# Two idle PSUM banks take the third and fourth down products; the routing runs unbroken on VectorE

## The reference

```python
def _L0_ffn_ref(x, Wr, br, Wgate, bgate, W1, W3, W2):    # x: (10000, 512), normed
    tw = _routing_weights(xf, Wr, br, Wgate, bgate)      # (N, 16)
    for e in range(16):                                  # W1, W3: 512 x 32, W2: 32 x 512
        h = silu(xf @ W1[e]) * (xf @ W3[e])
        out = out + tw[:, e:e + 1] * (h @ W2[e])

# _routing_weights: softmax over 4 groups, and in each group softmax over 4 experts;
# keep the top 2 of each (the second only while the cumulated share is <= 0.9),
# renormalise, multiply group by expert weight, times 0.5
```

## Time and profile before

| | |
|---|---|
| median of 3 runs | 2429.84 us |
| profiled execution, its own time | 2421.65 us |
| span of its instructions | 2419.9 us |
| PE busy | 2269.3 us (94%), 10550 matmuls |
| VectorE busy | 1794.4 us (74%) |
| ScalarE busy | 1150.4 us (48%) |
| GpSimd busy | 675.4 us (28%) |
| mean granted PE clock | 0.969 |

### The profile page before, as it was taken

How to read it: one execution, slowest core, us unless ns; L and a number is a source line. 1 busy time by engine, 2 the same in 40 slices (tenths; PEclk the granted TensorE clock), 3 DMA queues, 4 the chain that set the end, 5 groups by cost and what they waited for, 6 DMA issues and landing times. The chain is left out here.

```text
span 2419.9 us, 33046 instructions
## 1 busy us (share of the span) xinstructions
PE 2269.3 (94%) x10550; PEld 1815.3 (75%) x10550; DVE 1794.4 (74%) x4258; ACT 1150.4 (48%) x2136; POOL 675.4 (28%) x624
## 2 busy tenths in 40 slices
PE   6799986899999999999789999999997899999998
PEld 4577665688888888888668888888876677777776
DVE  8588796888888888886556755555566688888886
ACT  7565322445445454454442222222235767667652
POOL 6455022222122221210222221222233334333320
PEclk9899987999999999999899999999998899999999
DMA  5211133132231322311443344333356566666631
GB/s 166 60 54 53 19 127 104 60 98 89 69 105 60 99 88 70 105 53 49 158 161 126 125 146 134 129 129 133 130 160 202 112 181 153 148 175 159 152 109 48
DMA packets 155872, 271.87 MB, mean 112 GB/s; under 512 B 35538, under 2 KB 36178, under 8 KB 155478
## 3 DMA queue, kind: packets, MB, share of 16 engines
q1 hardware_dynamic: 123014, 203.00, 25.0%
q0 software_dynamic: 32720, 67.19, 12.8%
HBM read 185.82 MB, written 100.41 MB: 118 GB/s over the span
## 5 line engine op out<-in xcount | busy, mean ns | idle before, releaser
L2415 ACT ACTIVATE conv_h<-conv_h 128x512 f32<-128x512 f32 x79 | 50.0, 632 | 306.1 <-DVE conv_h L2344 306.1
L2892 POOL DMA_INDIRECT next_own<-message,net_slot_d x75 | 125.4, 1672 | 149.7 <-DMA next_own<-own 132.3
L2313 DVE TENSOR_TENSOR conv_yl<-conv_pty,conv_yh 128x512 fp32r<-128x512 f32 x79 | 54.6, 691 | 149.0 <-ACT conv_yh L2405 141.0
L68 PE MATMUL conv_p<-conv_w_hi,conv_yh 128*128 128x512 f32 x316 | 132.4, 419 | 1.6 <-DVE conv_yl L2313 1.6
L68 PE MATMUL d_po<-shared_wq_hi,d_hh 128*128 128x512 f32 x316 | 129.5, 410 | 2.6 <-DVE rows_rows L1523 0.2
L1373 POOL TENSOR_TENSOR d_rs<-d_ve,net_half_neg 128x4 f32<-128x4 f32 x37 | 37.3, 1007 | 337.0 <-DVE d_ve L1431 283.8
L68 PE MATMUL d_pc<-d_xh,shared_wv_hi 128*128 128x512 f32 (+1 forms) x320 | 128.6, 402 | 0.0
L68 PE MATMUL d_pa<-d_xh,xp_w_hi 128*128 128x512 f32 (+1 forms) x320 | 128.1, 400 | 0.0
L70 PE MATMUL conv_p<-conv_w_hi,conv_yl 128*128 128x512 f32 x316 | 126.5, 400 | 0.0
L69 PE MATMUL conv_p<-conv_w_lo,conv_yh 128*128 128x512 f32 x316 | 126.2, 399 | 0.0
L70 PE MATMUL conv_p<-conv_w_hi,conv_hl 128*128 128x512 f32 x316 | 125.6, 397 | 0.0
(11 more groups left out here) (621 smaller groups left out, 7173.4 us busy)
## 6 DMA issues: line engine op xcount, KB each, us to landing
conv_yin<-y SPq DMA_DIRECT2D x79, 256.0 KB, 2.7
h<-conv_h SPq DMA_DIRECT2D x79, 256.0 KB, 2.0
own<-xp_own_buf SPq DMA_DIRECT2D x79, 256.0 KB, 2.0
next_own<-own SPq DMA_DIRECT2D x79, 256.0 KB, 4.5
next_x<-y SPq DMA_DIRECT2D x79, 256.0 KB, 2.9
out<-d_res SPq DMA_DIRECT2D x79, 256.0 KB, 2.6
y<-d_y SPq DMA_DIRECT2D x78, 256.0 KB, 2.2
d_x<-in_x SPq DMA_DIRECT2D x10, 1024.0 KB, 7.4
```

The costliest lines, as they stand in the source:

```text
L68: te.matmul(out, lhs[0], rhs[0], start=first, stop=False, skip_group_check=True)
L2313: v.tensor_tensor(lo[:, t % 2, :], bank[t % 2][:], hi[:, t % 2, :].bitcast(F32), ALU.subtract)\
L2415: act_.activation(h[:, t, :], h[:, t, :], ACT.Relu).then_inc(h_made, 1)
L2892: pool.indirect_dma_start(own[n][:, t, :], None, k.message2[:, :], bass.IndirectOffsetOnAxis(ap=k.slot["d"][:, T * g + t:T * g + t + 1], a ...
```

## The change

The third and fourth tile's down products go to `pc[1]` and `pa[1]`. The down products of tiles 2 and 3 lose their wait for `back`; those of tiles 0 and 1 wait for `back` of the same tile of the group before; and `up` of chunk 1 with `w1` gets a wait for all four `back`s of the group before. On VectorE the routing is in one piece, apart from `front1` and `front1_end`, and the four `back`s follow.

```diff
+        down_bank = [po[0], po[1], pc[1], pa[1]]
...
-                v.scalar_tensor_tensor(x[u][:, t, :], x[u][:, t, :], 1.0, po[t % 2][:], ALU.mult, ALU.add,
+                v.scalar_tensor_tensor(x[u][:, t, :], x[u][:, t, :], 1.0, down_bank[t][:], ALU.mult, ALU.add,
                                        accum_out=row_sum[:, t:t + 1]).then_inc(x2_made, 1)
...
-                    def first_back():
-                        back(g, u, 0)
-                        if front:
-                            front1(i, c_ + 2)
-
-                    between = {7: first_back, 9: lambda: back(g, u, 1)}
-                    if front:
-                        between[15] = lambda: front1_end(g + 2)
-                    routing(g + 1, between)
-                    back(g, u, 2)
-                    back(g, u, 3)
+                    routing(g + 1, {7: lambda: front1(i, c_ + 2), 15: lambda: front1_end(g + 2)} if front else {})
+                    for t in range(T):
+                        back(g, u, t)
...
+                if name == "w1" and cc == 1 and g:
+                    pe.wait_ge(x2_made, 4 * g + 2)
...
-                    if cc == 0:
-                        pe.wait_ge(x2_made, 4 * g + t + 1)
+                    if cc == 0 and g and t < 2:
+                        pe.wait_ge(x2_made, 4 * g - 4 + t + 1 + 2)
                     pe.wait_ge(hl_made, 4 * g + cc + 1 + 2)
-                    last = split3(pe, po[t % 2][:], (hh[:, cc, sl], hl[:, cc, sl]),
+                    last = split3(pe, down_bank[t][:], (hh[:, cc, sl], hl[:, cc, sl]),
                                   (w["w2"][0][:, cc, :], w["w2"][1][:, cc, :]), cc == 0, cc == KC - 1)
```

## The result

The changed kernel took 2416.14 us in the median of four runs (2414.22 to 2418.13), against 2430.35 us for the kernel before on the same chip (2429.34 to 2432.61). The ratio is 0.9943, with an interval of 0.9930 to 0.9957. The medians differ by 14.2 us. The forecast was 2419.0 us, or -10.8.

The account below looks back on a forecast made before the run. PE was taken as the bound, busy 94% of the span and waiting for VectorE twice per group. Only those waits counted, -10.8 us, the other terms nothing: 2429.84 - 10.8 = 2419.0 us, range 2415.5 to 2424.5.

Parts of the forecast that it names:

- (a): First expert stage: PE's two waits per group at the down products of tiles 2 and 3 go, -10.8 us.
- (b): VectorE: without two `back`s the routing ends 1.2 us earlier; cost nothing, 1.1 us to spare at `turn_mix`.
- (c): VectorE: four `back`s in a row behind the routing cost nothing; 0.9 to 1.0 us idle left at `w3`.
- (d): PE's new wait at `up` of chunk 1 costs nothing; margin 2.2 us, about 0.8 us in the last group.
- (e): `pc[1]` and `pa[1]` bring no new wait; the skill's rule on cycling PSUM banks would make the stage slower.
- R3: Rival: the clock falls in the down products of tiles 2 and 3, 91 us slower, 2510; chance 0.01.
- (f): Next possible waits behind the change: the second transposes, waiting for a low half on VectorE, margin 1.1 us; priced at nothing.
- R1: Rival: the gain is lost again at the next wait; period stays 37.76 us, time 2429.8, half lost 2424; chance 0.08.
- R2: Rival: the new wait at `up` of chunk 1 decides beyond 2.2 us of VectorE delay, slower beyond 2.8; chance 0.03.
- R4: Rival: the stage's gain holds but another stage shifts by some microseconds, 2415 to 2424; chance counted within the forecast's 0.88.

Follow-up runs that it names:

- the banks alone: Against the kernel before: the new banks and waits, but VectorE's order as before, with two `back`s inside the routing; 2421.98 us, ratio 0.9974.
- the run with a delay: Changed kernel plus three chained memsets (1.97 us) on VectorE between the routing and the `back`s; 2421.68 us, ratio 0.9973 to the kernel before.
- six memsets of delay: Changed kernel plus six chained memsets (3.95 us) on VectorE between the routing and the `back`s; 2461.94 us, ratio 1.0138 to the kernel before.

## Why the prediction was right

(a) *The waits of `down`, -10.8 us.* The nineteen stretches sum to 107.7 us, where they were 118.9: -11.2. The stage in two pairs of traces: -11.1 and -11.5. The part that was in doubt, the 1.2 us of slower pace behind a hole, was given back too. The small rest is the pace itself: 5.67 / 25 = 0.2267 us for a start, where I had taken 0.2275. The experiments split the term: tile 3's wait is worth 0.21 us of the period, tile 2's the other 0.39 or so of 0.60. I had split it 0.12 and 0.39, and the rest as pace.

(b) *`back` out of the routing, 0, but needed.* Predicted margin at the turn 1.1 us, measured about 1.0. That it would otherwise be the next wait is shown by the banks alone, which kept half of the gain.

(c) *Four `back`s in a row, 0.* Idle time at `w3` 0.85 us, predicted 0.9 to 1.0.

(d) *The new wait, 0.* Margin read from the rows 809.19 - 807.06 = 2.1 us, by the delay 2.0, predicted 2.2. In the last group the run with a delay gives 0.6 us, my estimate was 0.8. The price beyond the margin was too low: 46 us for 1.98 us is 23 per microsecond and not 19, since the transposes add their own in each group, and the last group has the smaller margin and 2.5 us of low clock. For the same reason the delay from which the kernel is slower than before is less than my 2.8 us: 1.97 us of delay left it 6.9 us faster and 3.95 us made it 33 us slower, and a straight line between the two crosses at 2.3 us (an estimate).

(e) *The banks.* No wait for `pc` or `pa` at the down products, and the clock in the stage stayed at 1.00. R3 did not come. What the Trainium skill describes in "TensorE: Matmul & The Clock Gate", section "A second HAM failure mode: psum-queue depth-cycling", is not seen in this stage, with the down products spread over two more banks: no gaps between the groups of matmuls (5.67 us for 25 starts) and no fall of the clock.

(f) *What is late next.* Of the two next waits, the transposes stand closer than `up`: 1.8 us of delay on VectorE (1.97 less the 0.17 by which they were late), against 2.0. That is more than my 1.1 us. A delay there would first be taken up by the 0.85 us of idle time at `w3`, and 1.1 + 0.85 comes near it; no run separates the two.

R1 did not come in this version, yet the banks alone are just R1 by half. R2's point of decision was right within 0.2 us. What it left out is the clock, which adds some 2.6 us per group once PE waits for 4.2 us.

R4 is there in two forms. The part ahead of the first down product varied by 12 us between executions of equal code. It moves single spans more than medians: those of the kernel before stayed within 2.3 us in five sets of runs, those of the changed kernel within 4.1 us in three. And the part from the message stage to the end is 2.4 to 3.1 us shorter in the three executions of the changed kernel than in the two of before. Where it arises differs among them, partly in the number of low-clock matmuls at the message stage's start (22 in both of before; 13, 12 and 23 after). That number alone does not explain it, since the trace with 23 has the shortest end of all. This isn't settled: I can't say whether the changed kernel causes it. It would account for most of what the first comparison gave beyond the forecast, 14.2 us against 10.8. So the mechanism and its size were right in the stage, which gave 11.1 and 11.5 us; how near the total comes to the forecast is in part luck, since the three comparisons of medians gave 14.2, 13.0 and 9.9 us.

## What to carry to other kernels

Look for small holes in a PE that reads as 99% busy by the starts of its matmuls, and price each by the distance of starts, not by the load's idle time. Where a wait is moved behind other work, write down its margin in the ordinary group and in the shortest one: here 2.0 and 0.6 us. With six memsets of delay the shortest group waited longest, and was the only one behind whose wait the clock fell. A change of banks and a change of order can be halves of one thing: here one alone gave half the gain and the other alone cost 184 us.

## What the runs showed of the hardware

- In the busy part of the stage, a wait of PE of 4.2 or 7.7 us was followed by some 13 matmuls at the low level, one start every 0.43 us (granted clock 0.58 and 0.53 in the windows behind), about 2.6 us on top of the wait; in two groups by some 7. A wait of 3.2 us was followed by some 23 short ones (288 columns) at 0.24 us instead of 0.13, 2.5 us in all. Behind waits of 1.7 us, and behind one of 2.7 us, the starts went on at the full pace (granted clock 1.00 in windows behind both).
- At the stage's start, where PE was busy for only 8.5 of 16.5 us, the low level also stood behind a wait of 2.5 us (granted clock 0.59).
- A matmul behind a hole lasts 0.50 us in the rows instead of 0.39, and the next start comes 0.34 us later instead of 0.23: 0.11 us on top of the hole, as in the earlier trace rows.
- Three VectorE memsets of 128x512 in a chain cost 0.66 us each, 0.48 of work and 0.17 until the semaphore let the next one go.
- The part of equal code ahead of the first down product took 450.8 to 462.6 us in the five executions of the table.
